# Last stage of a fused block: operands loaded during attention, sigmoids and products reordered, mixes in PSUM, two selects moved

## Chip, cores and metric

The kernel runs on one core of one Trainium2 chip. The metric is the device time in microseconds (us) from the first to the last instruction of the program; lower is better. The times before are three runs of the same kernel, and one further execution was profiled.

## What is computed

The reference is a transformer block on x of shape (4, 2048, 512) in fp32: a layer norm with a modulation computed from a small conditioning vector, causal attention with 16 heads of 32 and a shared rotary part of 32, a gated residual, and then, in the last stage, a second layer norm and a channel-mixing layer with a token shift:

```python
attn = einsum(softmax(causal(scores)), v);  x = x + ga * (attn @ W_o)
h = layernorm(x) * (1 + cb) + sb
h_prev = shift h by one token (0 for the first token of a sequence)
xr = mu_r * h + (1 - mu_r) * h_prev
xk = mu_k * h + (1 - mu_k) * h_prev
r = sigmoid(xr @ W_r.T);  k = square(relu(xk @ W_k.T))
x = x + gb * r * (k @ W_v.T)
```

## The kernel before

Four programs run one after the other, each with its own barrier: setup, projection, attention, feedforward. Every engine's order is written out by hand, with semaphores between engines. A product of two fp32 matrices is made of three matmuls of a high and a low part each (`three_pass`, L59 to L61): high by high, high by low, low by high. The high part is a copy that rounds (made by ACT), the low part the difference (made by DVE or POOL).

**Attention** handles 16 units (4 groups of heads by 4 sequences). A unit has four blocks of 512 queries, j = 0 to 3, with 4, 8, 12 and 16 steps of 128 keys. Per step PE makes scores for four heads (L1005, L1006), ACT the exponentials (L853, into one of five `probs` buffers), PE the weighted values (L1012, two steps at a time, two steps later). POOL sets the future keys of the last four steps of a block to zero (`clear_future`, L929, the "select") and adds the exponentials of most steps into `sum_g` (L954, L957); PE then closes the block's denominators (`att_ps_d`, L1012) from `sum_g`. In block 2, step 8 and step 9 hold the first two selects, and PE waits for both before it takes step 8's and 9's weighted values. In between, PE also makes products for the next unit's row maxima (L991), which DVE reduces.

**Feedforward**, the last stage, turns W_r, W_k and W_v on PE, and splits all four weights into parts; then it walks 16 chunks of 512 tokens. In chunk n PE makes the products r (mix_r by W_r), o (attention by W_o of chunk n+1), k (mix_k by W_k), 16 transposes of the normalised rows of chunk n+1, and v (by W_v): four groups of 12 matmuls in each of r, o, k and v, on four PSUM banks in turn, so that a group waits until its bank was read. The other engines' steps in a chunk:

- ACT: four sigmoids of r (L1339), four copies `keep_x1` (L1329), squares and high parts of k, then the high copies of mix_r of the next chunk, four of the attention (L1317), and the high copies of mix_k (L1323).
- DVE: `attention_out` (L1195), layer norm statistics, relus (L1274), `normalise` (L1211); then `token_shift`: `modulate` (L1225, from the transposes' PSUM banks `ps_t`), `shift` (L1233), `mix` (L1241, into `mix_f` in SBUF) and `mix_low` (L1247), with `value_out` (L1279) between.
- POOL: the product with the gate (L1391), the residual (L1380), the inverse deviation (L1384), low parts of k (L1398), the sum of the output (L1402), low parts of the attention (L1374).
- SP issues every transfer. All loads of the last stage are issued after its barrier, and the gate's load (2 MB, L1154) stands behind four others.

## Time and profile before

| | |
|---|---|
| median of 3 runs | 3795.58 us (3789.31 to 3804.19) |
| profiled execution | 3801.18 us |
| its span, first to last instruction | 3799.4 us |
| mean granted clock of TensorE | 0.969 of full speed |
| busy: PE, DVE, POOL, ACT | 94%, 71%, 72%, 47% of the span |
| attention | until 2915 us of the span |
| last stage | 2915 us to the end |

The span and the time of the profiled execution differ by 1.8 us. Busy shares are means over stages; a matmul's shown end overlaps the next one's start.

### The profile page before, as it was taken

To read this page: it belongs to the slowest core of one execution; us is meant where nothing else is said; L and a number is where in the kernel's file an instruction comes from. 1 tells how busy PE (TensorE), PEld (TensorE's weight loads), DVE (VectorE), ACT (ScalarE), POOL (GpSimd) and SP (SyncE) were. 2 spreads that over 40 slices of the span, in tenths; PEclk is the share of its full clock that TensorE was granted. 3 is DMA by queue.
4 is the path that set the end of the run, shared out by engine and by line. 5 is a ranking of instruction groups with operands and counts; after the bars stand their busy time and mean duration, and the time that the engine had idled before them with its cause. 6 is when DMAs were issued, how large, how long until landed. Compare 5 with 4: busy or idle time off the path is not lost. (4 is left out here: it accounts for less than half of the span.)

```text
span 3799.4 us, 55720 instructions
## 1 busy us (share of the span) xinstructions
PE 3586.7 (94%) x19296; PEld 2423.5 (64%) x19296; DVE 2702.1 (71%) x5390; ACT 1800.5 (47%) x3401; POOL 2722.6 (72%) x1225
## 2 busy tenths in 40 slices
PE   7999979999999999999999999999996899999998
PEld 4777746666666666666666666666663677777776
DVE  5676667777777777777777777777761777777775
ACT  2433325555555555555555555555553333333332
POOL 1333248889889898898898898988986455555555
PEclk8999989999999999999999999999997899999999
DMA  5789753463553544634635635445322111111110
GB/s 182 249 274 301 258 135 79 104 143 76 112 128 78 128 102 100 131 81 106 133 78 107 140 76 119 109 95 128 81 46 98 53 54 66 66 56 66 55 55 33
DMA packets 232263, 425.77 MB, mean 112 GB/s; under 512 B 25332, under 2 KB 26868, under 8 KB 231928
## 3 DMA queue, kind: packets, MB, share of 16 engines
q1 hardware_dynamic: 231992, 423.10, 43.0%
q8 instruction: 117, 1.92, 0.2%
q14 instruction: 90, 0.74, 0.1%
q10 hardware_dynamic: 64, 0.02, 0.0%
HBM read 300.86 MB, written 121.65 MB: 111 GB/s over the span
## 5 line engine op out<-in xcount | busy, mean ns | idle before, releaser
L853 ACT ACTIVATE att_probs<-att_ps_s 128x512 f32<-128x512 f32 (+3 forms) x2560 | 1311.8, 536 | 1014.6 <-PE att_ps_s L1006 915.1
L957 POOL TENSOR_TENSOR att_sum_g<-att_sum_g,att_probs 128x2048 f32<-128x2048 f32 (+3 forms) x432 | 1665.5, 3855 | 57.3 <-ACT att_probs L853 6.9
L888 DVE TENSOR_REDUCE att_piece_max<-att_ps_m 128x1 f32<-128x512 f32 x1536 | 970.8, 683 | 281.1 <-PE att_ps_m L991 278.8
L1005 PE MATMUL att_ps_s<-att_q_a,att_k_a 128*128 128x512 f32 (+3 forms) x2560 | 959.6, 379 | 13.3 <-DMA att_q_b<-att_neg_max 9.2
L1006 PE MATMUL att_ps_s<-att_q_b,att_k_b 65*128 65x512 f32 (+3 forms) x2560 | 932.2, 368 | 0.0
L891 DVE CUSTOM_DVE_ANT_0 att_ps_m<-att_ps_m,mask_qk 128x128 f32<-128x128 f32 (+3 forms) x1024 | 487.4, 512 | 292.5 <-PE att_ps_m L991 276.6
L991 PE MATMUL att_ps_m<-att_k_a,att_q_a 128*128 128x512 f32 (+3 forms) x1840 | 663.3, 383 | 17.1 <-PEq L215 13.7
L1005 PEld LDWEIGHTS att_ps_s<-att_q_a,att_k_a 128*128 128x128 f32 x2560 | 486.4, 190 | 195.1 <-issue 91.1
L1012 PE MATMUL att_ps_o<-att_probs,att_v 128*32 128x512 f32 (+3 forms) x5120 | 561.3, 546 | 32.7 <-POOL att_probs L929 32.7
L1006 PEld LDWEIGHTS att_ps_s<-att_q_b,att_k_b 65*128 65x128 f32 x2560 | 485.7, 190 | 61.2
L991 PEld LDWEIGHTS att_ps_m<-att_k_a,att_q_a 128*128 128x128 f32 x1840 | 348.5, 191 | 235.8 <-issue 105.1
L954 POOL TENSOR_TENSOR att_sum_g<-att_probs 128x1536 f32<-128x1536 f32 (+1 forms) x64 | 276.1, 4314 | 173.0 <-PE att_ps_d L1012 173.0
L1012 PEld LDWEIGHTS att_ps_o<-att_probs,att_v 128*32 128x32 f32 x5120 | 133.9, 110 | 296.3 <-issue 148.6
L901 DVE RECIPROCAL att_ps_d<-att_ps_d 128x128 f32<-128x128 f32 x256 | 224.3, 926 | 91.0 <-PE att_ps_d L1012 91.0
L991 PE MATMUL att_ps_m<-att_k_next,att_q_a 128*128 128x128 f32 (+1 forms) x720 | 256.8, 385 | 0.0
L1402 POOL TENSOR_TENSOR ffn_x_kept<-ffn_x_kept,ffn_gate_r 128x512 f32<-128x512 f32 x64 | 100.5, 1570 | 162.8 <-DVE ffn_gate_r L1279 162.8
L929 POOL TENSOR_SCALAR_AFFINE_SELECT att_probs<-att_probs 128x512 f32<-128x512 f32 x256 | 160.7, 636 | 66.3 <-ACT att_probs L853 66.2
L991 PEld LDWEIGHTS att_ps_m<-att_k_next,att_q_a 128*128 128x128 f32 x720 | 134.3, 190 | 99.8 <-issue 37.7
L1195 DVE TENSOR_TENSOR ffn_x<-ffn_ps_ffn,ffn_gate 128x512 f32<-128x512 f32 x64 | 44.2, 691 | 176.3 <-PE ffn_ps_ffn L61 150.7
L1345 ACT ACTIVATE ffn_act_f<-ffn_relu 128x512 f32<-128x512 f32 x64 | 40.4, 632 | 262.2 <-DVE ffn_relu L1274 261.5
L459 POOL TENSOR_TENSOR prj_h_lo<-prj_h_f,prj_h_hi 128x512 fp32r<-128x512 f32 x64 | 80.5, 1292 | 106.4 <-ACT prj_h_hi L404 106.4
L59 PE MATMUL ffn_ps_ffn<-ffn_w_o_hi,ffn_att_hi 128*128 128x512 f32 x256 | 111.6, 436 | 40.9 <-ACT ffn_gate_r L1339 35.4
(173 smaller groups left out, 5096.8 us busy)
## 6 DMA issues: line engine op xcount, KB each, us to landing
att_q_a<-s_q_hi SPq DMA_DIRECT2D x128, 256.0 KB, 6.0
att_q_a<-s_qr_hi SPq DMA_DIRECT2D x128, 256.0 KB, 7.1
prj_x_sb<-in_x_dram SPq DMA_DIRECT2D x16, 1024.0 KB, 5.3
s_q_hi<-prj_q_hi SPq DMA_DIRECT2D x16, 1024.0 KB, 4.4
s_q_lo<-prj_q_lo SPq DMA_DIRECT2D x16, 1024.0 KB, 6.5
s_k_hi<-prj_k_hi SPq DMA_DIRECT2D x16, 1024.0 KB, 4.5
s_k_lo<-prj_k_lo SPq DMA_DIRECT2D x16, 1024.0 KB, 6.5
s_v<-prj_v_sb SPq DMA_DIRECT2D x16, 1024.0 KB, 9.3
```

What stands on the lines that cost most here:

```text
L59: mm(out, stat[0], mov[0], start=first, stop=False)
L853: act.activation(probs[t % RING][:, hh, c0:CH], ps_s[(GH * t + hh) % SBANKS][:, c0:CH], ACT.Exp, scale=SCALE).then_inc(probs_ready, 1)
L888: dve.tensor_reduce(top, ps_m[:, bank, :], AX_X, ALU.max).then_inc(piece_taken, 1)
L891: dve.tensor_tensor_reduce(ps_m[:, bank, 0:width], ps_m[:, bank, 0:width], keep["mask_qk"][:, CH - width:CH], 1.0, MASKED, ALU.add, ALU.ma ...
L901: dve.reciprocal(cols, cols).then_inc(rden_ready, 1)
L929: pool.affine_select(out=at, in_=at, compare_op=ALU.is_ge, fill=0.0, base=0, pattern=[[0, GH], [1, P]], channel_multiplier=-1).then_inc(cl ...
L954: pool.tensor_tensor(sum_g[:, :, c0:CH], first[:, :, c0:CH], new, ALU.add).then_inc(sum_added, 1)
L957: pool.tensor_tensor(sum_g[:, :, c0:CH], sum_g[:, :, c0:CH], new, ALU.add).then_inc(sum_added, 1)
L991: mm(ps_m[:, bank, 0:width], q_a[j][:, hh, r * P:(r + 1) * P], keys, start=True, stop=True).then_inc(piece_ready, 1)
L1005: mm(out[:, c0:CH], k_a[:, hh, i * P:(i + 1) * P], q_a[j][:, hh, c0:CH], start=True, stop=False)
L1006: last = mm(out[:, c0:CH], k_b[:, hh, i * P:(i + 1) * P], q_b[j][:, hh, c0:CH], start=False, stop=True)
L1012: last = mm(out[hh * HD:(hh + 1) * HD, c0:CH], stat(hh), mov[:, hh, c0:CH], start=start, stop=stop, skip_group_check=True)
```

## The change

1. The four weights of the last stage and the first chunk's attention are loaded by SP during the last unit of attention, into the places of query buffers that this unit no longer needs (`raw_views`, `load_for_last_stage`). Parts of the weights and of the mixes are then kept in attention's operand buffers (keys, queries), so that all fits.
2. The start of the last stage is reordered: W_o is split in four pieces beside the attention's four, PE makes the first two o groups before it turns W_k, and the gate is loaded in four pieces, the first one first.
3. `modulate` goes from DVE to ACT. `mix` writes into `ps_t` (banks 0 and 1 for r, 2 and 3 for k) instead of SBUF.
4. The sigmoids stand between the high copies of mix_k, and no longer wait for the last chunk's output sums; `value_out` writes into the buffers of the relus and squares (`gated`) instead of `gate_r`. The relus and squares take over the wait on those sums.
5. In block 2 of attention, POOL's sum of step 7 stands behind the selects of steps 8 and 9.

```diff
+            def load_for_last_stage(j):
+                wait_alone(sp, scores_ready, GH * (NSTEP * (NU - 1) + FIRST[j] + STEPS[j]), sp_mark)
+                if j == 0:
+                    wait_alone(sp, o_stored, 16 * (TCH * (NU - 2)), sp_mark)
+                    sp.dma_start(ops["raw"]["att"][:], scratch["o"].rearrange("(g n) p t -> n p g t", g=NG)[0]).then_inc(ops["att_in"], 16)
+                    load_weight(0)
+                    load_weight(3)
+                else:
+                    load_weight(j)
...
+                else:
+                    load_for_last_stage(0)
...
+                else:
+                    load_for_last_stage(1)
...
+                else:
+                    load_for_last_stage(2)
...
+                    mine = [n for n, o in enumerate(SHARE_OF[j]) if o == "G"]
+                    order = [(what, i) for i in range(STEPS[j]) for what in ("clear", "add")]
+                    if j == 2:
+                        order.remove(("add", TB * j - 1))
+                        order.insert(order.index(("clear", TB * j + 1)) + 1, ("add", TB * j - 1))
+                    for what, i in order:
+                        if what == "clear" and i >= TB * j:
+                            wait_alone(pool, probs_ready, heads_ready(u, FIRST[j] + i, GH - 1), pool_mark)
                             clear_future(u, j, i)
...
+                        if what == "add" and i in mine[1:]:
+                            add(u, j, i, mine)
...
+        w_o, w_r = ([ops["k_a"][:, k, :].rearrange("p (c n) -> p c n", c=NC) for k in two] for two in ((0, 1), (2, 3)))
+        w_k = ops["k_next"], sb("w_k_lo", [P, NC, D], F32R)
...
+        mix_r, mix_k = (ops["q_a"][0], ops["q_a"][1]), (ops["q_a"][2], ops["q_b"][0])
...
+        w_raw = [ops["raw"][n] for n in ("w_o", "w_r", "w_k", "w_v")]
+        first_att = ops["raw"]["att"]
...
+        gated = [relu[:, 0, :], relu[:, 1, :], act_f[:, 0, :], act_f[:, 1, :]]
...
+            def load_gate(b):
...
+            load_gate(0)
             sp.dma_start(x_sb[:], x_v[0]).then_inc(x_in, 16)
-            sp.dma_start(gate[:], scratch["gate"][None].broadcast_to([P, NB, 2, D])).then_inc(gate_in, 16)
-            load_weight(3)
             sp.dma_start(mu[:, 0, :], dram["mu_r"].rearrange("(c p) -> p c", p=P), allow_slow_non_contiguous=True).then_inc(mu_in, 16)
             sp.dma_start(mu[:, 1, :], dram["mu_k"].rearrange("(c p) -> p c", p=P), allow_slow_non_contiguous=True).then_inc(mu_in, 16)
-            sp.wait_ge(att_lo, NG)
             sp.dma_start(att_f[:], att_v[1]).then_inc(att_in, 16)
+            for b in range(1, NB):
+                load_gate(b)
             sp.wait_ge(x1_ready, TB)
...
+            def output_weight_low(c):
+                dve.wait_ge(wo_hi, c + 1)
+                dve.tensor_tensor(w_o[1][:, c, :], w_raw[0][:, c, :], as_f32(w_o[0][:, c, :]), ALU.subtract).then_inc(wo_lo, 1)
...
-            def modulate(n, c):
-                dve.wait_ge(t_ready, NC * n + c + 1)
-                dve.tensor_scalar(h2[:, c, 1:1 + CH], ps_t[:, c, :], keep["mod"][:, 3, c, bass.ds(n, 1)],
-                                  keep["mod"][:, 2, c, bass.ds(n, 1)], ALU.mult, ALU.add).then_inc(h2_ready, 1)
...
-                dve.scalar_tensor_tensor(out=mix_f[:, c % 2, j, :], in0=diff[:, c, :], scalar=mu[:, j, c:c + 1],
+                dve.scalar_tensor_tensor(out=ps_t[:, 2 * j + c % 2, :], in0=diff[:, c, :], scalar=mu[:, j, c:c + 1],
...
-                dve.tensor_tensor(dst[1][:, c, :], mix_f[:, c % 2, j, :], as_f32(dst[0][:, c, :]),
+                dve.tensor_tensor(dst[1][:, c, :], ps_t[:, 2 * j + c % 2, :], as_f32(dst[0][:, c, :]),
...
-                modulate(n, 0)
                 for c in range(NC):
-                    if c + 1 < NC:
-                        modulate(n, c + 1)
                     shift(n, c)
...
                     dve.wait_ge(actf_ready, NC * n + m - 1)
+                else:
+                    dve.wait_ge(y_ready, TB * n + 1)
                 dve.tensor_scalar(relu[:, m % 2, :], ps[:, m, :], 0.0, None, ALU.max).then_inc(taken[m], 1)
...
+                dve.tensor_tensor(gated[m], ps[:, m, :], gate_r[:, m, :], ALU.mult).then_inc(taken[m], 1)
...
-            weight_low(0)
+            for c in range(NC):
+                output_weight_low(c)
             weight_low(1)
+            dve.wait_ge(gate_in, 16)
+            attention_out(0, range(0, 2))
             weight_low(2)
-            dve.wait_ge(gate_in, 16)
-            attention_out(0)
+            attention_out(0, range(2, TB))
...
+            dve.wait_ge(gate_rest, 16 * (NB - 1))
...
+            def modulate(n):
+                act.wait_ge(carry_ready, n + 2)
+                for c in range(NC):
+                    act.wait_ge(t_ready, NC * n + c + 1)
+                    act.activation(h2[:, c, 1:1 + CH], ps_t[:, c, :], ACT.Identity, scale=keep["mod"][:, 3, c, bass.ds(n, 1)],
+                                   bias=keep["mod"][:, 2, c, bass.ds(n, 1)]).then_inc(h2_ready, 1)
+
+            def gate(n, m):
+                act.wait_ge(*ready(f"r{m}", n))
+                act.activation(gate_r[:, m, :], ps[:, m, :], ACT.Sigmoid).then_inc(taken[m], 1)
...
+                    act.copy(dst[0][:, c, :], ps_t[:, 2 * j + c % 2, :]).then_inc(mix_hi[j], 1)
...
-                for m in range(TB):
-                    act.wait_ge(*ready(f"r{m}", n))
-                    act.wait_ge(y_ready, TB * n + 1)
-                    act.activation(gate_r[:, m, :], ps[:, m, :], ACT.Sigmoid).then_inc(taken[m], 1)
+                for c in range(NC):
+                    mix_high(n, 1, c)
+                    if c:
+                        gate(n, c - 1)
+                gate(n, TB - 1)
...
                 if nxt:
+                    modulate(n + 1)
                     mix_high(n + 1, 0)
                     if after:
                         act.wait_ge(*ready("v3", n))
                         split_attention(n + 2)
-                    mix_high(n + 1, 1)
...
+            act.wait_ge(att_in, 16)
+            for g in range(NG):
+                act.copy(att[0][:, g, :], first_att[:, g, :]).then_inc(att_hi, 1)
+                act.copy(w_o[0][:, g, :], w_raw[0][:, g, :]).then_inc(wo_hi, 1)
+            act.wait_ge(att_lo, NG)
...
+            modulate(0)
             mix_high(0, 0)
             act.wait_ge(grp_ready, 4)
             split_attention(1)
-            mix_high(0, 1)
...
-            pool.wait_ge(gate_in, 16)
-            low_attention(0)
+            low_attention(0, first_att)
...
+            def attention_out(n, reuse, part=range(TB)):
+                if reuse:
+                    pe.wait_ge(att_lo, NG * n + NG)
+                for m in part:
                     if reuse:
                         pe.wait_ge(*bank_free(f"o{m}", n - 1))
                     for c in range(NG):
+                        if not reuse and m == 0:
+                            pe.wait_ge(att_lo, c + 1)
+                            pe.wait_ge(wo_lo, c + 1)
...
-            pe.wait_ge(w_lo, 4)
+
+            turn_weight(1)
+            attention_out(0, False, range(0, 2))
+            turn_weight(2)
+            attention_out(0, False, range(2, TB))
+            turn_weight(3)
+            pe.wait_ge(w_lo, 3)
```

POOL in attention, block 2 of one unit, from the block's first sum on. Before:

```order
L954 TENSOR_TENSOR att_sum_g<-att_probs 128x2048
L957 TENSOR_TENSOR att_sum_g<-att_sum_g,att_probs 128x2048 x6
L929 AFFINE_SELECT att_probs<-att_probs 128x4x128 x2
L957 TENSOR_TENSOR att_sum_g<-att_sum_g,att_probs 128x4x384
L929 AFFINE_SELECT att_probs<-att_probs 128x4x128
L957 TENSOR_TENSOR att_sum_g<-att_sum_g,att_probs 128x4x256
L929 AFFINE_SELECT att_probs<-att_probs 128x4x128
L957 TENSOR_TENSOR att_sum_g<-att_sum_g,att_probs 128x4x128
```

Now:

```order
L982 TENSOR_TENSOR att_sum_g<-att_probs 128x2048
L985 TENSOR_TENSOR att_sum_g<-att_sum_g,att_probs 128x2048 x5
L966 AFFINE_SELECT att_probs<-att_probs 128x4x128 x2
L985 TENSOR_TENSOR att_sum_g<-att_sum_g,att_probs 128x2048
L985 TENSOR_TENSOR att_sum_g<-att_sum_g,att_probs 128x4x384
L966 AFFINE_SELECT att_probs<-att_probs 128x4x128
L985 TENSOR_TENSOR att_sum_g<-att_sum_g,att_probs 128x4x256
L966 AFFINE_SELECT att_probs<-att_probs 128x4x128
L985 TENSOR_TENSOR att_sum_g<-att_sum_g,att_probs 128x4x128
```

The two selects of 128x4x128 have gone ahead of one full sum.

ACT in the last stage, from the head of the loop over chunks to the end of the sigmoids. Before (the first row is the last in front of the loop, and the same at the end of its body):

```order
L1323 CAST ffn_mix_k_hi<-ffn_mix_f 128x512 x4
L1364 UNCONDITIONAL_BRANCH
L1364 ISA
L1338 ISA
L1339 ACT_TABLE_LOAD
L1339 ACTIVATE ffn_gate_r<-ffn_ps_ffn 128x512
L1337 REGISTER_ALU
L1339 ACTIVATE ffn_gate_r<-ffn_ps_ffn 128x512
L1337 REGISTER_ALU
L1339 ACTIVATE ffn_gate_r<-ffn_ps_ffn 128x512
```

Now, where `att_q_a<-ffn_ps_t` is the high copy of mix_k:

```order
L1422 UNCONDITIONAL_BRANCH
L1422 ISA
L1375 ACT_TABLE_LOAD
L1375 CAST att_q_a<-ffn_ps_t 128x512
L1374 REGISTER_ALU
L1375 CAST att_q_a<-ffn_ps_t 128x512
L1368 ISA
L1369 ACT_TABLE_LOAD
L1369 ACTIVATE ffn_gate_r<-ffn_ps_ffn 128x512
L1374 REGISTER_ALU
L1375 CAST att_q_a<-ffn_ps_t 128x512
L1368 REGISTER_ALU
```

The copies of mix_k have come from the end of the loop's body to its head, the sigmoids stand between them, and there are two loads of a function table where there was one.

DVE in the loop, the first part of `token_shift`. Before:

```order
L1225 ISA
L1225 TENSOR_SCALAR ffn_h<-ffn_ps_t,mod 128x512
L1225 ISA
L1225 TENSOR_SCALAR ffn_h<-ffn_ps_t,mod 128x512
L1233 TENSOR_TENSOR ffn_diff<-ffn_h 128x512
L1241 SCALAR_TENSOR_TENSOR ffn_mix_f<-ffn_diff,ffn_mu,ffn_h 128x512
L1225 ISA
L1225 TENSOR_SCALAR ffn_h<-ffn_ps_t,mod 128x512
L1233 TENSOR_TENSOR ffn_diff<-ffn_h 128x512
L1247 TENSOR_TENSOR ffn_mix_r_lo<-ffn_mix_f,ffn_mix_r_hi 128x512
L1241 SCALAR_TENSOR_TENSOR ffn_mix_f<-ffn_diff,ffn_mu,ffn_h 128x512
```

Now:

```order
L1272 TENSOR_TENSOR ffn_diff<-ffn_h 128x512
L1280 SCALAR_TENSOR_TENSOR ffn_ps_t<-ffn_diff,ffn_mu,ffn_h 128x512
L1272 TENSOR_TENSOR ffn_diff<-ffn_h 128x512
L1286 TENSOR_TENSOR att_q_a<-ffn_ps_t,att_q_a 128x512
L1280 SCALAR_TENSOR_TENSOR ffn_ps_t<-ffn_diff,ffn_mu,ffn_h 128x512
L1315 REGISTER_ALU
L1317 TENSOR_TENSOR ffn_relu<-ffn_ps_ffn,ffn_gate_r 128x512
```

The modulations (L1225) have left DVE's order, and the mixes go to `ffn_ps_t`.

## Rows read from the trace of the kernel before

**Rows 1.** Timeline, block 2 of one unit of attention: start, duration, engine, operation, [idle before].

```profile
1907.50 1.07 PE L1012 MATMUL att_ps_d<-att_sum_g,ones 128*32 128x512 f32 x8 [0.36 <-POOL att_sum_g L957]
...
1913.47 28.26 POOL L957 TENSOR_TENSOR att_sum_g<-att_sum_g,att_probs 128x2048 f32<-128x2048 f32 x6
...
1931.69 4.56 ACT L853 ACTIVATE att_probs<-att_ps_s 128x512 f32<-128x512 f32 x8 [2.37 <-PE att_ps_s L1006]
...
1941.69 1.22 POOL L929 TENSOR_SCALAR_AFFINE_SELECT att_probs<-att_probs 128x512 f32<-128x512 f32 x2
1942.38 1.06 PE L1012 MATMUL att_ps_o<-att_probs,att_v 128*32 128x512 f32 x8 [1.75 <-POOL att_probs L929]
...
1950.18 1.29 POOL L957 TENSOR_TENSOR att_sum_g<-att_sum_g,att_probs 128x512 f32<-128x512 f32 x1
...
1953.10 1.07 PE L1012 MATMUL att_ps_d<-att_sum_g,ones 128*32 128x512 f32 x8
```

**Rows 2.** Timeline of PE, that wait in four of fifteen units, first and last included.

```profile
758.30 1.41 PE L1012 MATMUL att_ps_o<-att_probs,att_v 128*32 128x512 f32 x8 [1.74 <-POOL att_probs L929]
...
1054.52 1.06 PE L1012 MATMUL att_ps_o<-att_probs,att_v 128*32 128x512 f32 x8 [1.74 <-POOL att_probs L929]
...
1201.84 1.21 PE L1012 MATMUL att_ps_o<-att_probs,att_v 128*32 128x512 f32 x8 [1.78 <-POOL att_probs L929]
...
2838.41 1.94 PE L1012 MATMUL att_ps_o<-att_probs,att_v 128*32 128x512 f32 x8 [1.77 <-POOL att_probs L929]
```

**Rows 3.** Window: engines' busy us, granted clock, DMA share, GB/s.

```profile
2835.00:2840.00 5.00, 3.23 (x19) 1.72 (x23) 0.50 (x2) 1.83 (x7) 4.92 (x4) 0.76 0.01 2
```

**Rows 4.** Chain that ended last and timeline, start of the last stage.

```profile
2915.02 0.39 SPq L1146
...
2919.25 17.71 DMA ffn_gate<-s_gate
...
2937.03 4.94 POOL L1374 TENSOR_TENSOR ffn_att_lo<-ffn_att_f,ffn_att_hi 128x512 fp32r<-128x512 f32 x4 [30.67 <-DMA ffn_gate<-s_gate]
...
2963.69 3.64 PE L1446 MATMUL ffn_ps_t<-ident_f,ffn_diff 128*128 128x128 f32 x16 [6.25 <-DVE ffn_diff L1211]
```

**Rows 5.** Timeline of PE, one chunk of the last stage.

```profile
3062.89 1.91 PE L1446 MATMUL ffn_ps_t<-ident_f,ffn_diff 128*128 128x128 f32 x16
...
3075.82 0.39 PE L59 MATMUL ffn_ps_ffn<-ffn_w_r_hi,ffn_mix_r_hi 128*128 128x512 f32 x1
...
3080.38 0.50 PE L59 MATMUL ffn_ps_ffn<-ffn_w_r_hi,ffn_mix_r_hi 128*128 128x512 f32 x1 [2.20 <-DVE ffn_mix_r_lo L1247]
...
3088.68 0.39 PE L59 MATMUL ffn_ps_ffn<-ffn_w_r_hi,ffn_mix_r_hi 128*128 128x512 f32 x1
...
3091.76 0.48 PE L59 MATMUL ffn_ps_ffn<-ffn_w_o_hi,ffn_att_hi 128*128 128x512 f32 x1 [2.24 <-ACT ffn_gate_r L1339]
...
3113.94 1.91 PE L1446 MATMUL ffn_ps_t<-ident_f,ffn_diff 128*128 128x128 f32 x16
```

**Rows 6.** Timeline of PE, transposes of the second and the last chunk.

```profile
3010.50 1.91 PE L1446 MATMUL ffn_ps_t<-ident_f,ffn_diff 128*128 128x128 f32 x16
...
3740.64 1.91 PE L1446 MATMUL ffn_ps_t<-ident_f,ffn_diff 128*128 128x128 f32 x16
```

**Rows 7.** Timelines of DVE, ACT and POOL, same chunk.

```profile
3075.39 1.78 DVE L1247 TENSOR_TENSOR ffn_mix_r_lo<-ffn_mix_f,ffn_mix_r_hi 128x512 fp32r<-128x512 f32 x1
...
3083.36 6.82 POOL L1374 TENSOR_TENSOR ffn_att_lo<-ffn_att_f,ffn_att_hi 128x512 fp32r<-128x512 f32 x4
...
3089.72 1.28 ACT L1339 ACT_TABLE_LOAD   x1
3091.01 2.07 ACT L1339 ACTIVATE ffn_gate_r<-ffn_ps_ffn 128x512 f32<-128x512 f32 x4
```

**Rows 8.** Groups by line, 3000 to 3700 us: count, busy us, mean ns.

```profile
L1225 DVE TENSOR_SCALAR ffn_h<-ffn_ps_t,mod 128x512 f32<-128x512 f32 x56 | 43.9, 805 | 2.9 <-DVE ffn_h L1219 2.9
...
L1279 DVE TENSOR_TENSOR ffn_gate_r<-ffn_ps_ffn,ffn_gate_r 128x512 f32<-128x512 f32 x53 | 36.0, 679 | 0.0
```

More of the change, by code:

```diff
@@ L668, in operand_loads, with attention @@
     return load_q_a, load_q_b, load_k_a, load_k_b, load_v, (heads, rotary)
-def attention(nc, keep, scratch, ops):
+def attention(nc, keep, scratch, ops, dram):
     with ExitStack() as ctx:
@@ L680, in attention @@
         k_b = sb("k_b", [2 * HD + 1, GH, T], F32R)
-        ops["q_a"] += [sb(f"q_a{j}", [P, GH, CH], F32R) for j in range(2, TCH)]
+        ops["q_a"].append(sb("q_a3", [P, GH, CH], F32R))
         ops["q_b"] += [sb(f"q_b{j}", [2 * HD + 1, GH, CH], F32R) for j in range(1, TCH)]
@@ L1428, in token_rows @@
                 last.then_inc(grp_ready, 1)
-            def attention_out(n, reuse):
-                pe.wait_ge(att_lo, NG * n + NG)
-                for m in range(TB):
+            def attention_out(n, reuse, part=range(TB)):
+                if reuse:
+                    pe.wait_ge(att_lo, NG * n + NG)
+                for m in part:
                     if reuse:
@@ L1525, in adaln_block @@
                 projection(nc, keep, dram, scratch, prj, ops)
-            attention(nc, keep, scratch, ops)
-        feedforward(nc, keep, dram, scratch, out)
+            late_operands(nc, held, ops)
+            ops["raw"] = raw
+            attention(nc, keep, scratch, ops, dram)
+            feedforward(nc, keep, dram, scratch, out, ops)
 _INS = {
```

115 lines of the change are left out of this document (56 added, 59 removed).

## The prediction

> **What bounds the kernel now.** I read three stretches in the timeline, each for the wait that PE ends last, since PE is busy nearly everywhere else.
>
> First, attention. In every unit from the second on, PE stands still for 1.75 us in front of the weighted values of block 2's steps 8 and 9, released by POOL's select [rows 1, 2]; there are fifteen such waits, from 758.30 to 2838.41. POOL came to the selects late because it had six full sums to make first (28.26 us). The exponentials that the selects need were done at 1931.69 + 4.56 = 1936.25, long before the select at 1941.69. The mean distance of two such waits is (2838.41 - 758.30) / 14 = 148.6 us, but 1201.84 - 1054.52 = 147.3 where the clock held. In most units the granted clock falls around this wait (0.76 in one window [rows 3]), that is, part of it goes at 1.2 instead of 2.4 GHz, and the same eight matmuls take up to 1.94 instead of 1.06 us [rows 1, 2].
>
> Second, the start of the last stage. From its first transfer at 2915.02 to the first chunk's transposes at 2963.69 it takes 48.7 us [rows 4]. The chain of waits shows why: the gate's transfer took 17.71 us behind the weights, POOL waited for it before the attention's low parts (4.94 us), and only then did PE begin the products o.
>
> Third, the chunks. From the second chunk's transposes to the last one's, 3010.50 to 3740.64, are 14 periods of 52.15 us [rows 6]. In the chunk shown [rows 5] the period is 3113.94 - 3062.89 = 51.05. The r groups run from 3075.82 to the last triple's end at 3088.68 + 0.69, that is 13.55 us, where 16 triples without a wait take 11.1 (o and k together, 32 triples, take 3113.94 - 3091.76 = 22.2): 2.45 lost, waiting for mix_r's low part on DVE. Then o starts at 3091.76 instead of 3089.37: 2.4 lost, waiting for the sigmoid, which ACT starts only behind all copies of mix_k and a table load of 1.28 us [rows 7]. Without both the chunk takes 46.2 us. The other 1.1 us of the mean are longer waits of the same two kinds and the lower clock after them.
>
> **The change, part by part.** The sum is made against the profiled execution's own 3801.2 us.
>
> *Selects in block 2.* POOL's sixth full sum is put behind the selects. The full sum lasts 28.26 / 6 = 4.7 us, so the selects start at about 1937.0, when the exponentials are 0.8 us old: POOL loses nothing, and the selects are over at 1938.3, two us before PE asks (1942.38 - 1.75 = 1940.6). The stall of 1.75 goes. Next is late what closes block 2: POOL's last sum ends at 1950.18 + 1.29 = 1951.5, PE's closing product was at 1953.10 and would now be at 1951.35, so PE waits there as it does for block 1 (0.36 [rows 1]). Net 1.75 - 0.35 = 1.4 by 15 units = 21 us. The clock: 148.6 - 147.3 = 1.3 us a unit, 19 us in all; it goes if the falls hang on this stall, and I take nine tenths, 17. Together **38 us**. The bounds are 5 (if POOL's sums set the pace all through) and 45.
>
> *Loads during attention.* Five transfers of 1 MB go into the last unit, where the DMA engines are idle (share 0.01 [rows 3]). SP issues them where it otherwise loads the next unit's queries, so they stand ahead of two stores and two small loads of row maxima that other units have behind larger loads. Cost nothing; if this cover were gone, at most the gate's 17.7 us of one transfer queue.
>
> *Start of the last stage.* From 2915: four pairs of copies on ACT at 0.55 us (2.07 / 4 [rows 7]) end at 2919.7, POOL's low parts of the attention at about 2920.5 (4.94 in sequence), while PE turns W_r. The o products, which began at 2942, can begin at 2919.2: 22.8 us earlier. What followed them took 21.7 us until the transposes, and now has W_k's turning in it as well (1.9 us [rows 5], the copy and difference behind it lie beside the next products). I take 2942.7, **21 us** earlier. Bounds 15 (the gate's first quarter or SP's slow small loads of mu late) and 24.
>
> *Chunks, DVE.* Four modulations of 0.80 us leave the stretch that gates r [rows 8]. The low parts now read one operand from PSUM: with two operands in SBUF they took 1.78 us while a POOL sum ran [rows 7], with PSUM on one side, as in value_out, the mean of 53 is 0.68 whatever POOL did [rows 8]. I followed the order by hand from the transposes (T): mix 0 is ready at T + 4.3; each further step is shift, low, mix and value_out at 0.6 to 0.7 each, plus some 0.6 of waiting for POOL, 3.3 in all; the last low part ends at T + 14.4. PE needs it at T + 12.9 + 2.1 = 15.0 (transposes and v, 3075.82 - 3062.89 [rows 5], and three quarters of the first r group). The stall closes, with 0.6 us to spare. For a modulation on ACT the nearest row, the sigmoids from PSUM, has 2.07 / 4 = 0.52 us [rows 7]; the upper bound is DVE's 0.80 [rows 8]. Four of them start when ACT is through with the squares of k, about 2.3 us into the transposes, and only the first is waited for. The Trainium skill (ScalarE: Activation LUTs, What ACT_TABLE_LOAD costs) adds some 93 ns for each of the two pointer operands; by that it is 0.79, no more than the upper bound.
>
> *Chunks, ACT and POOL.* The sigmoid of r0 now follows the second copy of mix_k. The copies run at T + 18.9 and T + 19.7, the table load ends at T + 21, the sigmoid at T + 21.6; PE comes to o at T + 12.9 + 11.1 = 24.0. No wait. What is late next is POOL: it adds the last output sum at T + 19 or so and then makes four low parts of the attention, which took 6.82 us with DVE in between [rows 7] and about 5.9 with fewer DVE operations of two SBUF operands. That gives T + 24.2 to 25, so I leave 0.2 to 1.0 us of waiting. Row maxima of mix_k, relus and squares keep their distances to k, which has 11 us in hand; the store of the last output has some 6 us to land before `keep_x1`. Period 46.2 + 0.6 = 46.8 us; 14 periods save 5.35 each, **75 us**. Bounds: 5.95 each (83 us) and 1.5 each (21 us).
>
> A rule weighed here: the row shows the table load at 1.28 us and the sigmoids starting at once behind it, at 3091.01 [rows 7]. The order now has two such loads per chunk, 2.6 us of ACT. The Trainium skill (same page and section) counts 2.66 us for every switch of sets, the drain included. By the row the sigmoid has 2.4 us in hand before o; by the page it would come 2.8 us later, o would wait 0.4 us and the 14 periods save some 6 us less.
>
> *Ends.* The first chunk gains about 1.5 us (shorter steps on DVE), the last one its wait for mix_r of the same kind as above and the clock behind it, 3 us. Together **4.5 us**.
>
> Sum: 38 + 21 + 75 + 4.5 = 138.5, so 3801.2 - 138.5 = 3662.7. The median of the runs lies 5.6 us below the profiled execution: **3657 us**, 3.6% faster.
>
> **Rivals.**
>
> *A, POOL becomes the wait in the chunks.* POOL's low parts of the attention follow the output sum, which follows value_out of v3, which DVE reaches late, and every DVE operation with two SBUF operands stretches POOL's. For it speaks that POOL ended at 3083.36 + 6.82 = 3090.2, only 1.6 us before o was released by the sigmoid; against it that DVE gets there earlier. If PE waits 2.5 us each chunk and the clock takes 0.5 more, a period is 49.2: 41 us instead of 75, and the time 3691.
>
> *B, the selects bring nothing.* POOL is the pace of block 2 and its closing eats the stall: 5 us instead of 38, time 3690. For it speaks that closings of block 1 already wait for POOL; against it that this wait is 0.36 and that PE had 1.6 us in hand at block 2's [rows 1].
>
> *C, both*: 3724.
>
> *D, slower: ACT holds r back.* Modulations and copies of mix_r are now in one line on ACT, behind the squares of k. If its operations on PSUM banks that DVE writes were so slow that the chain of four modulations and four copies grew, PE would wait for mix_r in every chunk. The other terms give 63.5 us; to be slower by 0.5% (19 us) the chunks have to lose 82.5 / 14 = 5.9 us each against now, so the chain has to be some 12 us longer than I have it, 1.5 us for each of its eight operations. That would give 3815. The rows show 0.5 to 0.8 for such operations.
>
> *E, no change over 0.5%*: the waits only change their names, period and units alike; 3780 to 3795.
>
> **How the numbers follow.** Chances: forecast 0.60 (its own range 3632 to 3680), A 0.18, B 0.12, C 0.05, D 0.03, E 0.02. The predicted time is that of the forecast, 3657. The low end takes all upper bounds, 45 + 24 + 83 + 6 = 158: 3801.2 - 158 - 5.6 = 3637.6, and a little for the scatter of the runs, 3634. The high end takes in A and B with some margin and stops short of C: 3706. Below 0.5% (19 us) the runs of this kernel, which differ by 15 us, could hardly tell a change. Faster by more than that: forecast and A to C, 0.95; same 0.02; slower 0.03.
>
> **What would show it.** PE's wait before `att_ps_o` in block 2 is gone in units 2 to 16, and one of 0.3 us stands before `att_ps_d` of block 2; the distance of units is 146 us with the clock at full speed there. The first transposes of a chunk come 28 us behind the start of the last stage. The periods of the transposes are 46 to 47.5 us, and the wait before o, if any, names POOL's low parts of the attention, not the sigmoid. Wrong would be: a wait for mix_r still over 1 us in each chunk (my steps on DVE), a wait named after ACT's modulations, POOL standing idle in front of block 2's selects, or clock falls in other places of attention.

## The result, and the profile after

The changed kernel takes 3670.07 us (median of 4 runs, 3669.48 to 3673.73), and the kernel before, run beside it, 3792.44 us: a ratio of 0.9674, 95% interval 0.9651 to 0.9698. The profiled execution took 3669.48 us (span 3667.7), 131.7 us less than that of before; the prediction had 138.5.

The page of the changed kernel, busy time by engine and the granted clock in 40 slices:

```profile
PE 3536.2 (96%) x19296; PEld 2400.9 (65%) x19296; DVE 2577.7 (70%) x5329; ACT 1855.2 (51%) x3482; POOL 2711.1 (74%) x1225
...
PEclk8999979999999999999999999999999899999999
```

The timeline of block 2 of the unit shown in [rows 1], POOL and PE, from the closing of block 1 to that of block 2:

```profile
1903.96 1.06 PE L1054 MATMUL att_ps_d<-att_sum_g,ones 128*32 128x512 f32 x8 [0.36 <-POOL att_sum_g L985]
...
1905.20 4.61 POOL L982 TENSOR_TENSOR att_sum_g<-att_probs 128x2048 f32<-128x2048 f32 x1 [1.38 <-PE att_ps_d L1054]
1909.95 23.55 POOL L985 TENSOR_TENSOR att_sum_g<-att_sum_g,att_probs 128x2048 f32<-128x2048 f32 x5
1933.44 1.23 POOL L966 TENSOR_SCALAR_AFFINE_SELECT att_probs<-att_probs 128x512 f32<-128x512 f32 x2
1934.63 8.20 POOL L985 TENSOR_TENSOR att_sum_g<-att_sum_g,att_probs 128x2048 f32<-128x2048 f32 x2
...
1945.84 0.64 POOL L966 TENSOR_SCALAR_AFFINE_SELECT att_probs<-att_probs 128x512 f32<-128x512 f32 x1
1946.54 0.43 PE L1054 MATMUL att_ps_o<-att_probs,att_v 128*32 128x128 f32 x8 [1.04 <-POOL att_probs L966]
...
1947.89 1.06 PE L1054 MATMUL att_ps_d<-att_sum_g,ones 128*32 128x512 f32 x8 [0.43 <-POOL att_sum_g L985]
...
1949.13 4.60 POOL L982 TENSOR_TENSOR att_sum_g<-att_probs 128x2048 f32<-128x2048 f32 x1 [1.30 <-PE att_ps_d L1054]
```

The wait of 1.75 us ahead of steps 8 and 9 is gone. Two others stand in its place, 1.04 us for the select of step 11 and 0.43 for the last sum, and between 1905.20 and the last sum POOL is never idle. In the kernel before POOL wasn't idle there either. Its timeline of a unit in which the clock held shows PE closing 0.05 us behind the last sum (1062.36 + 1.28), and the same 1.30 us between that sum and the next block:

```profile
1020.83 4.61 POOL L954 TENSOR_TENSOR att_sum_g<-att_probs 128x2048 f32<-128x2048 f32 x1 [1.38 <-PE att_ps_d L1012]
...
1062.36 1.28 POOL L957 TENSOR_TENSOR att_sum_g<-att_sum_g,att_probs 128x512 f32<-128x512 f32 x1
1063.69 1.07 PE L1012 MATMUL att_ps_d<-att_sum_g,ones 128*32 128x512 f32 x8
1064.94 4.60 POOL L954 TENSOR_TENSOR att_sum_g<-att_probs 128x2048 f32<-128x2048 f32 x1 [1.30 <-PE att_ps_d L1012]
```

I measure block 2 below from its first sum on POOL to that of block 3: 1064.94 - 1020.83 = 44.11 us here, 43.93 after. Over fifteen units (all but the first) before had 44.1 us in four and 45.0 to 46.9 in eleven (mean 45.35); after has 43.9 to 44.3 in thirteen and 44.8 in two (mean 44.10).

The start of the last stage and the chunks, timeline of SP's queue and PE, answering to [rows 4, 6]:

```profile
2898.74 0.33 SPq L1191 DMA_DIRECT2D ffn_gate<-s_gate  x1
...
2902.09 0.78 PE L59 MATMUL ffn_ps_ffn<-att_k_a,ffn_att_hi 128*128 128x512 f32 x1
...
2926.16 3.65 PE L1509 MATMUL ffn_ps_t<-ident_f,ffn_diff 128*128 128x128 f32 x16 [6.25 <-DVE ffn_diff L1255]
...
2970.02 1.91 PE L1509 MATMUL ffn_ps_t<-ident_f,ffn_diff 128*128 128x128 f32 x16
...
3613.23 1.91 PE L1509 MATMUL ffn_ps_t<-ident_f,ffn_diff 128*128 128x128 f32 x16
```

From first transfer to first transposes are 27.4 us (48.7 before), and a period of the chunks is (3613.23 - 2970.02) / 14 = 45.94 us (52.15 before). PE has no wait left in these 14 periods, and the granted clock is 1.00 in all of them. One chunk on ACT, POOL and PE, in timelines as [rows 7]:

```profile
3077.47 1.28 ACT L1375 ACT_TABLE_LOAD   x1
3078.76 1.07 ACT L1375 CAST att_q_a<-ffn_ps_t 128x512 fp32r<-128x512 f32 x2
3079.65 5.94 POOL L1432 TENSOR_TENSOR ffn_att_lo<-ffn_att_f,ffn_att_hi 128x512 fp32r<-128x512 f32 x4
3079.85 1.28 ACT L1369 ACT_TABLE_LOAD   x1
3081.15 0.60 ACT L1369 ACTIVATE ffn_gate_r<-ffn_ps_ffn 128x512 f32<-128x512 f32 x1
...
3085.73 0.42 PE L59 MATMUL ffn_ps_ffn<-att_k_a,ffn_att_hi 128*128 128x512 f32 x1
...
3110.03 2.78 ACT L1364 ACTIVATE ffn_h<-ffn_ps_t,mod 128x512 f32<-128x512 f32 x4
```

and DVE's groups by line over the chunks (2970 to 3613 us), the low parts of mix_r and mix_k:

```profile
L1286 DVE TENSOR_TENSOR att_q_a<-ffn_ps_t,att_q_a 128x512 fp32r<-128x512 f32 x56 | 38.4, 685 | 1.7
L1286 DVE TENSOR_TENSOR att_q_b<-ffn_ps_t,att_q_a 128x512 fp32r<-128x512 f32 x56 | 38.3, 684 | 11.8 <-ACT att_q_a L1375 10.9
```

POOL's low parts end at 3079.65 + 5.94 = 3085.59, 0.14 us before PE begins the products o at 3085.73.

### The profile page after: what moved, and what is told of

Its sections match the earlier page's. It is cut to its first block and busy times, and to the rows that moved or that the text cites. A ratio compares the mean times of both kernels' runs of the same rounds, so it can differ in the third digit from the quotient of the medians.

```text
span 3667.7 us, 55764 instructions
## 1 busy us (share of the span) xinstructions
PE 3536.2 (96%) x19296; PEld 2400.9 (65%) x19296; DVE 2577.7 (70%) x5329; ACT 1855.2 (51%) x3482; POOL 2711.1 (74%) x1225
## 3 DMA queue, kind: packets, MB, share of 16 engines
q1 hardware_dynamic: 232424, 423.10, 44.1%
## 5 line engine op out<-in xcount | busy, mean ns | idle before, releaser
L1033 PE MATMUL att_ps_m<-att_k_a,att_q_a 128*128 128x512 f32 (+3 forms) x1840 | 663.7, 383 | 17.0 <-PEq L215 13.7
L1239 DVE TENSOR_TENSOR ffn_x<-ffn_ps_ffn,ffn_gate 128x512 f32<-128x512 f32 x64 | 44.1, 691 | 159.7 <-PE ffn_ps_ffn L61 159.7
L928 DVE DVE_READ_ACCUMULATOR2_ANT att_piece_max<- 128x1 f32 x1024 | 144.1, 141 | 0.0
L1456 POOL TENSOR_TENSOR ffn_att_lo<-ffn_act_f,ffn_att_hi 128x512 fp32r<-128x512 f32 x64 | 86.0, 1354 | 68.1 <-ACT ffn_att_hi L1385 68.1
```

The costliest lines, as they stand in the source:

```text
L928: dve.tensor_tensor_reduce(ps_m[:, bank, 0:width], ps_m[:, bank, 0:width], keep["mask_qk"][:, CH - width:CH], 1.0, MASKED, ALU.add, ALU.ma ...
L1033: mm(ps_m[:, bank, 0:width], q_a[j][:, hh, r * P:(r + 1) * P], keys, start=True, stop=True).then_inc(piece_ready, 1)
```

## Where the 131.7 us are

| stretch | predicted | measured | from |
|---|---|---|---|
| attention, from unit 1's block 3 to the end | 38 | 18.3 | 2293.6 and 2275.3 us |
| ahead of that | 0 | -2.0 | block 3 of unit 1 starts at 621.45 before, 623.49 after |
| start of the last stage | 21 | 21.3 | 48.7 and 27.4 us |
| 14 periods | 75 | 86.9 | 52.15 and 45.94 us |
| first and last chunk | 4.5 | 7.2 | 46.8 and 43.9; 58.8 and 54.5 us |

The 2.0 us ahead aren't the change's: that block started between 621.4 and 623.8 us in all executions profiled, whatever they contained.

My theory of attention (P) from here on: POOL's chain of sums and selects sets the pace of block 2, before and after; moving the selects only moves PE's pause, and what it gained is the clock. The rivals are the prediction's step (PE sets the pace) and C (the clock falls have another cause).

## The experiments

Ratios are against the kernel before, run on the same chip; "from the changed kernel" compares medians of separate sets of runs.

| run | median us | ratio, 95% interval | from the changed kernel |
|---|---|---|---|
| select_only (on before) | 3774.09 | 0.9952, 0.9936 to 0.9967 | |
| select_back | 3692.46 | 0.9722, 0.9691 to 0.9752 | +22 |
| last_selects | 3675.01 | 0.9683, 0.9657 to 0.9709 | +5 |
| step11_on_pe | 3635.81 | 0.9582, 0.9557 to 0.9606 | -34 |
| step11_only | 3653.53 | 0.9622, 0.9584 to 0.9659 | -17 |
| modulate_dve | 3692.21 | 0.9737, 0.9710 to 0.9765 | +22 |
| mix_sbuf | 3711.41 | 0.9788, 0.9760 to 0.9816 | +41 |
| sigmoids_last | 3672.88 | 0.9686, 0.9658 to 0.9713 | +3 |
| both_back | 3729.84 | 0.9826, 0.9788 to 0.9864 | +60 |
| all_back | 3761.38 | 0.9905, 0.9875 to 0.9935 | +91 |
| loads_late | 3680.28 | 0.9707, 0.9679 to 0.9734 | +10 |
| gate_whole | 3671.70 | 0.9674, 0.9636 to 0.9713 | +2 |

### The selects alone, and the selects back

select_only is the kernel before with POOL's order of the change (the functions `add` and `body` of the diff) and nothing else. select_back is the changed kernel without it:

```diff
-                    if j == 2:
-                        order.remove(("add", TB * j - 1))
-                        order.insert(order.index(("clear", TB * j + 1)) + 1, ("add", TB * j - 1))
```

> The kernel before with only the order of POOL in block 2 changed (the sum of step 7 behind the selects of steps 8 and 9). Theory P, POOL's chain of sums and selects (42.6 us from its first sum) sets the pace of block 2, and only the clock falls hang on the order: block 2, from POOL's first sum to that of block 3, takes 43.95 us in nearly all units instead of 44.1 to 46.9, PE waits some 1.1 us for the select of step 11 and 0.4 for the last sum, and the time is 18 us below the kernel before (2 for the stall, 16 for the clock). The prediction's own step, PE was the pace and the stall falls away: 38 us below. Rival C, the clock falls come from elsewhere and were gone in the changed kernel for another reason: 2 us below, with falls in most units.

> The changed kernel with only the order of POOL in block 2 put back (sum of step 7 ahead of the selects). Theory P: the 1.75 us stall before steps 8 and 9 is back, block 2 takes 44.1 us where the clock holds and 45.3 to 46.9 where it falls, 16 to 20 us above the changed kernel, all of it in attention; the chunks stay at 45.94 us. The prediction's step: 38 us above. Rival C (the falls have another cause): 2 us above.

select_only came 20.8 us below the median of before, block 2 at 43.95 to 43.98 us in twelve of fifteen units (mean 44.11, before 45.35: 15 x 1.24 = 18.6 us). Its timeline has the two small waits of the changed kernel:

```profile
1946.10 0.43 PE L1017 MATMUL att_ps_o<-att_probs,att_v 128*32 128x128 f32 x8 [1.07 <-POOL att_probs L929]
...
1947.45 1.06 PE L1017 MATMUL att_ps_d<-att_sum_g,ones 128*32 128x512 f32 x8 [0.44 <-POOL att_sum_g L948]
```

select_back lost 22 us, and block 2 was back at 45.3 to 46.8 in thirteen units (mean 45.85). The prediction's step (38 each way) and C (2) are out. P fits: 18 expected and 20.8 measured without the other edits, 16 to 20 expected and 22 measured among them. In select_back's trace the clock fell in fourteen of the fifteen units, where before it had in eleven. The windows of select_back around one of its pauses, engines' busy time, granted clock, DMA share and GB/s, show the clock's part:

```profile
1650.00:1655.00 5.00, 3.32 (x24) 2.11 (x26) 1.08 (x4) 2.36 (x8) 4.92 (x4) 0.79 0.31 88
1655.00:1660.00 5.00, 5.00 (x24) 1.66 (x17) 0.00 (x0) 0.03 (x1) 4.92 (x3) 0.53 1.06 210
```

In the second window PE is busy throughout (5.00 of 5 us), at little more than half of the full clock (0.53).

### The pause moved, and POOL relieved

last_selects also exchanges the select of step 11 with the sum of step 10; step11_only leaves that order and gives the sum of step 11 to PE; step11_on_pe does both.

```diff
+                        order.remove(("add", TB * j + 2))
+                        order.insert(order.index(("clear", TB * j + 3)) + 1, ("add", TB * j + 2))
```

```diff
-SHARE_OF = ("GGTT", "GGGGGGGG", "GGGGGGGGTGGG", "GGGGGGTGGGGGTGGG")
+SHARE_OF = ("GGTT", "GGGGGGGG", "GGGGGGGGTGGT", "GGGGGGTGGGGGTGGG")
```

> The changed kernel with one more pair of POOL's operations in block 2 exchanged: the select of step 11 ahead of the sum of step 10. POOL's work in the block is the same, so theory P expects block 2 at 43.95 us as in the changed kernel: the wait of 1.08 us at the select goes, and PE waits 1.5 us for the last sum instead (now 0.44). If the clock holds, the time is that of the changed kernel within 3 us. If one pause of 1.5 us in one piece is what lets the clock fall (it was 1.75 us before, in one piece), falls come back in many units and the time is up to 16 us above. The rival that this select's place costs PE time by itself: 1.1 us a unit less, 16 us below.

> As the run with the last selects exchanged, and in addition the sum of step 11 of block 2 is made by PE (four products of 128 columns, some 0.25 us) and not by POOL (1.29 us). Theory P: block 2 gets 1.2 to 1.3 us shorter, 42.7 us, PE's waits shrink to 0.3 us or less, and 15 or 16 units give 19 us, so 19 us below the changed kernel. The rival that PE is the pace of block 2 (the prediction's step): 4 us above the changed kernel.

> The changed kernel with the sum of step 11 of block 2 on PE, but the selects in the changed kernel's order (select of step 11 behind the sum of step 10). Theory P: PE still waits about 1 us for that select, but closes right behind: block 2 takes 43.2 us (43.95 in the changed kernel, 42.47 with both edits), and the 0.75 us a unit that block 3 got shorter through the new deal of the maxima stays. Together 1.4 to 1.5 us a unit, 22 us below the changed kernel, 12 above the kernel with both edits. The rival that the whole gain of the kernel with both edits comes from the sum's place and the deal: 34 us below.

last_selects: the select's wait is gone, and the closing waits instead, in one piece of 1.61 to 1.70 us in nine of the fifteen units (0.57 to 1.27 in the five before them, 3.29 in the last):

```profile
1945.40 1.06 PE L1056 MATMUL att_ps_d<-att_sum_g,ones 128*32 128x512 f32 x8 [1.66 <-POOL att_sum_g L985]
```

Block 2 takes 43.9 us where the clock holds, as without the exchange, so the same work on POOL gives the same time wherever PE pauses. The clock fell behind this closing in five units, and in two of them block 3 took 65.8 us for 62.8. These 6 us are about what the kernel lost (5 us).

step11_on_pe shows who sets the pace. POOL has a sum of 1.28 us less, PE the second row below more, and block 2 takes 42.47 us, 1.5 less. PE comes to the closing just when POOL is done (1200.11 + 2.38 = 1202.49) and closes without a wait:

```profile
1200.11 2.38 POOL L985 TENSOR_TENSOR att_sum_g<-att_sum_g,att_probs 128x1024 f32<-128x1024 f32 x1
...
1201.78 0.40 PE L1056 MATMUL att_ps_d<-att_probs,ones 128*32 128x128 f32 x8
...
1202.55 1.07 PE L1056 MATMUL att_ps_d<-att_sum_g,ones 128*32 128x512 f32 x8
```

The direction is P's, the size wasn't: 34 us for 19. Block 2 gave 23.3 us over fifteen units. The rest is block 3, 62.05 for 62.8 us, 0.75 in each unit, although POOL and PE do the same work there. The share table (`SHARE_OF`, which engine sums which step) also feeds the plan that deals the products for the row maxima to the steps, and in the new deal one of them stands between two heads of step 1 of block 3, where PE before followed ACT's pace. That this is the cause is read from the timelines only, no run has the new deal alone. step11_only has the shorter block 3 too (62.1), without the exchange. Its block 2 takes 43.58 us (I had 43.2), and it gains 17 us for the 22 that I expected, since PE still waits 0.93 us for the select of step 11:

```profile
1205.62 0.43 PE L1054 MATMUL att_ps_o<-att_probs,att_v 128*32 128x128 f32 x8 [0.93 <-POOL att_probs L966]
```

So both edits count, and their worth hangs on POOL's chain: the exchange of step 11's select costs 5 us by itself, and on top of the shorter chain it brings 18. step11_on_pe is 0.9% faster than the changed kernel and the fastest version I have.

### The chunks: modulation, mixes, sigmoids

Each run undoes one part of the changed kernel.

```diff
             def token_shift(n, meanwhile):
+                modulate(n, 0)
                 for c in range(NC):
+                    if c + 1 < NC:
+                        modulate(n, c + 1)
                     shift(n, c)
```

is modulate_dve, with `modulate` as in the kernel before. mix_sbuf writes and reads the mixes in a buffer of their own:

```diff
-                    act.copy(dst[0][:, c, :], ps_t[:, 2 * j + c % 2, :]).then_inc(mix_hi[j], 1)
+                    act.copy(dst[0][:, c, :], mix_f[:, 2 * j + c % 2, :]).then_inc(mix_hi[j], 1)
```

and so in `mix` and `mix_low`. sigmoids_last has `gate_r` for `gated`, and:

```diff
-                for c in range(NC):
-                    mix_high(n, 1, c)
-                    if c:
-                        gate(n, c - 1)
-                gate(n, TB - 1)
+                mix_high(n, 1)
+                act.wait_ge(y_ready, TB * n + 1)
+                for m in range(TB):
+                    gate(n, m)
```

> The changed kernel with the modulation put back on DVE (one ahead of each shift, as before). My step order: DVE's stretch from the transposes to the last low part of mix_r gets four modulations of 0.7 to 0.8 us more and starts 0.4 us earlier, less 0.8 us of waiting that they fill, so the last low part comes about 1.5 to 2 us later; it has 0.7 us in hand, so PE waits about 1 us for it in each chunk and the period grows from 45.94 to about 47 us: 15 us above the changed kernel. In addition the attention's low parts on POOL, which end 0.1 us before PE begins the products o, shift with DVE's value_out, but PE shifts as well. The rival that the modulation's move is the largest part of the chunks' gain: 3 us each, period 49, 43 us above. The rival that it brings nothing beside the mixes in PSUM: 0.

> The changed kernel with the mixes kept in SBUF and not in the PSUM banks of the transposes, so that each low part has two SBUF operands. If such an operation waits for the whole operation of POOL that runs beside it (1.78 us in the trace of before against 0.68 with one PSUM operand), each of the four low parts of mix_r takes 0.5 to 1.1 us longer: 3 us later at the end, of which 0.7 are in hand, so PE waits 2.3 us before r in each chunk, and POOL, held up too, comes later with the attention's low parts by some 1 us: period 48.5 us, 36 us above the changed kernel, with clock falls. If the two operands don't matter: period 45.94, no change.

> The changed kernel with the sigmoids put back behind all four copies of mix_k, into the buffer that value_out then overwrites, behind the wait for the last output sum. The copies now come earlier than in the kernel before: the fourth ends 13.1 us before the next transposes minus 35.2, that is 21.9 us behind the chunk's transposes, the table load ends at 23.2 and the first sigmoid at 23.8, when PE is through with r at 23.9 (0.1 us in hand). My theory: PE waits 0 to 0.3 us, period 45.9 to 46.2, 0 to 4 us above the changed kernel, so the place of the sigmoids brings next to nothing once the mixes come early. The prediction's reading (a part of 2.4 us a chunk hangs on this order): 34 us above.

Periods: 47.39, 48.82 and 46.15 us against 45.94, that is 1.45, 2.88 and 0.21 us a chunk. I had 1, 2.5 and 0 to 0.3, so the first two are dearer than expected, and the clock falls that I expected with the mixes in SBUF didn't come (1.00 in all 14 periods). In the timelines PE waits, with the modulation on DVE, 0.55 us for mix_r and 0.33 for POOL's low parts; with the mixes in SBUF:

```profile
3132.96 0.50 PE L59 MATMUL ffn_ps_ffn<-att_k_a,att_q_a 128*128 128x512 f32 x1 [1.56 <-DVE att_q_a L1287]
...
3142.83 0.50 PE L59 MATMUL ffn_ps_ffn<-att_k_a,ffn_att_hi 128*128 128x512 f32 x1 [0.74 <-POOL ffn_att_lo L1433]
```

The reason stands in mix_sbuf's groups by line (2970 to 3650 us), the same low parts with both operands in SBUF, and POOL's low parts of the attention beside them:

```profile
L1287 DVE TENSOR_TENSOR att_q_b<-ffn_mix_f,att_q_a 128x512 fp32r<-128x512 f32 x56 | 93.8, 1694 | 3.6 <-ACT att_q_a L1376 3.6
L1287 DVE TENSOR_TENSOR att_q_a<-ffn_mix_f,att_q_a 128x512 fp32r<-128x512 f32 x56 | 85.0, 1518 | 2.4
```

```profile
L1433 POOL TENSOR_TENSOR ffn_att_lo<-ffn_att_f,ffn_att_hi 128x512 fp32r<-128x512 f32 x56 | 95.6, 1737 | 0.0
```

Only the place of one operand differs, and the instruction takes 1518 to 1694 ns for 685, POOL's 1737 for the 1518 of the changed kernel. It isn't that SBUF is slow to read: the same instruction is short where POOL is idle and long where POOL runs, here in one chunk of mix_sbuf:

```profile
3121.92 0.69 DVE L1287 TENSOR_TENSOR att_q_a<-ffn_mix_f,att_q_a 128x512 fp32r<-128x512 f32 x1
...
3123.95 1.68 POOL L1461 TENSOR_TENSOR ffn_x_kept<-ffn_x_kept,ffn_relu 128x512 f32<-128x512 f32 x1 [4.06 <-DVE ffn_relu L1318]
3124.39 1.79 DVE L1287 TENSOR_TENSOR att_q_a<-ffn_mix_f,att_q_a 128x512 fp32r<-128x512 f32 x1
```

Over thirteen chunks mix_r's low parts take 0.69 us the 13 times that POOL is idle and 1.78 to 1.82 the 39 times that it runs; in the changed kernel, with one operand in PSUM, they take 0.67 to 0.69 either way. The Trainium skill (SBUF — State Buffer, Who interferes with whom) has this as a rule: a DVE instruction with two SBUF inputs contends with a GpSimd instruction that reads SBUF, and one with a single SBUF input, outside its two-port modes, doesn't. The trace agrees, with these numbers. The sigmoids' place is worth 0.21 us by itself, as the copies of mix_k now come early.

### The same parts, undone together

both_back undoes modulation and mixes, all_back the sigmoids too, with the same edits.

> The changed kernel with both edits on DVE's side undone, the modulation on DVE and the mixes in SBUF; the sigmoids stay between the copies of mix_k. Alone the two cost 1.45 and 2.88 us a chunk (periods 47.39 and 48.82 against 45.94). Theory S, one chain through DVE with 0.7 us in hand: the delays add up and the slack is only paid once, so both together cost about 1.45 + 2.88 + 0.7 = 5.0, period 51.0 us, 70 us above the changed kernel, unless the clock falls, which adds up to 1. The rival that the edits stand in for each other (either would do): 48.8 to 49.3.

> As the run with modulation and mixes put back, and the sigmoids behind all copies of mix_k too: the chunk schedule of the kernel before on top of the other edits. Theory S: since the copies of mix_k are late now, the sigmoid is late for the products o, and what was worth 0.2 us alone is worth 1 to 2 here: period 52.1 us as in the kernel before (52.15), with clock falls in most chunks. The rival that the order of the sigmoids is worth 0.2 everywhere: period as in the run with the sigmoids between the copies, plus 0.2.

both_back has a period of 49.84 us, 3.90 above the changed kernel; the single losses add to 4.33. So the parts don't stand in for each other, and the slack doesn't count once more on top, as I had expected (51.0). Five of its periods hold a clock fall (50.2 to 51.1 us); the other nine take 49.5, 3.6 above. Why the two together cost less than their sum isn't shown. all_back has 52.10 us, near the kernel before's 52.15, so the other edits bring nothing to a chunk. The sigmoids' order is worth 52.10 - 49.84 = 2.26 us here and 0.21 in the changed kernel: PE's wait in all_back's timeline is the one of [rows 5], longer:

```profile
3107.26 0.47 PE L59 MATMUL ffn_ps_ffn<-att_k_a,ffn_att_hi 128*128 128x512 f32 x1 [3.27 <-ACT ffn_gate_r L1378]
```

The chunk of [rows 5] isn't the common one. In the kernel before PE waits for mix_r either 1.1 or 2.2 us, and o begins 28.8 us behind the transposes in thirteen of the 14 periods whichever it was: the sigmoid sets that moment, and a longer first wait only makes the second one shorter. Nor do the two waits add to more in any other period than to the 4.4 us of that chunk. What lifts the mean to 52.15 is the clock: twelve of the 14 periods hold a fall, and [rows 5] shows one of the other two.

### The start of the last stage

loads_late issues them in the last stage's queue, and none in attention:

```diff
+            load_weight(1)
+            load_weight(0)
+            sp.dma_start(first_att[:], att_v[0]).then_inc(att_in, 16)
             load_gate(0)
+            load_weight(2)
             sp.dma_start(x_sb[:], x_v[0]).then_inc(x_in, 16)
+            load_weight(3)
```

gate_whole loads the gate at once, in the place of `load_gate(0)`:

```diff
+                sp.dma_start(gate[:], scratch["gate"][None].broadcast_to([P, NB, 2, D])).then_inc(gate_in, 16)
...
-            for b in range(1, NB):
-                load_gate(b)
```

> The changed kernel with the first attention rows and the four weights loaded at the start of the last stage and not in the last attention unit; the gate still comes in parts, and POOL doesn't wait for it. W_r, W_o and the attention rows need 3 MB; their transfers took 5.6, 8.4 and 8 us from issue to landing in the trace of before, one behind the other, so the products o begin about 11 us behind the start of the stage and not 3.3: the stretch from its first transfer to the first transposes grows from 27.4 to about 35 to 37 us, 8 to 10 us above the changed kernel. The rival that the loads' early place is worth the whole 21 us: 48 us, 21 above. The rival that only POOL's wait for the gate mattered: 28 us, no change.

> The changed kernel with the gate loaded in one transfer of 2 MB and not in four of 512 KB. DVE needs the gate for the first two o groups 11.7 us behind the start of the stage (2910.40 against 2898.74); the whole gate took 17.7 us in the trace of before behind 4 MB of others, and here has the queue to itself at first: some 10 to 14 us. So DVE comes up to 2 us late for o0, which must be taken for the residual, not for PE's next products; x and the small loads of mu land later too, and the last token shift waits for mu. First transposes 27.4 to 31 us behind the start, 0 to 4 us above the changed kernel. The rival that the split carries the start's gain: 17.7 us for the gate, 6 us or more.

loads_late: from its first transfer at 2896.24 to the first transposes at 2934.75 are 38.5 us, 11.1 more (I had 35 to 37 us); o begins 13.7 us in and not 3.3. The last unit of attention takes 148.9 us from its first sum without the loads and 149.7 with them, so they cost attention little (0.8 us between these two runs). Its timeline of PE:

```profile
2901.90 3.67 PE L1530 MATMUL ffn_ps_t<-ident_f,raw_w_r 128*128 128x128 f32 x16 [12.36 <-DMA raw_w_r<-in_w_r_dram]
2909.96 0.77 PE L59 MATMUL ffn_ps_ffn<-att_k_a,ffn_att_hi 128*128 128x512 f32 x1 [4.38 <-DVE att_k_a L1216]
```

gate_whole: 2923.38 - 2895.95 = 27.4 us, no change. So of the 21.3 us at the start 11 hang on the loads in attention. The other 10 are left for POOL no longer waiting for the gate and for the order of the steps; no run parts these two. With the loads in attention, one piece of the gate or four makes no difference.

## Why the prediction held, and where it didn't

**The time** was in the range, 13 us above the predicted one. Against the profiled executions I was 6.8 us off, and that is luck in part: the selects were 19.7 us too high, the periods and the ends together 14.6 too low. The rest of the 13 is mostly the 5.6 us by which I put the median under the profiled execution of before; the changed kernel's runs lie within 4 us, and its median 0.6 above its profiled execution.

**Selects in block 2** is the step that failed: 38 us predicted, 18.3 measured. Its clock part was right (17; block 2 got 45.35 - 44.10 = 1.25 us shorter on average, 0.13 where the clock held, so 15 x 1.12 = 17 are the clock's). Its stall part was "Net 1.75 - 0.35 = 1.4 by 15 units = 21 us", and it is 2. It rests on "PE had 1.6 us in hand at block 2's [rows 1]": POOL's last sum ended at 1951.5 and PE closed at 1953.10. But that row is from a unit in which the clock had fallen behind the stall, and PE was late for that reason. In the four units with the clock up PE closes 0.05 us behind POOL's last sum, before as after (1063.69 above): PE had nothing in hand. I took the clock's loss once as clock and once as slack. Rival B, which I gave 0.12, had the mechanism right and the price wrong, for it gave up the clock's gain too. Both runs of the selects and step11_on_pe show it. "POOL loses nothing" was right, and for that reason the move could give nothing.

**Loads during attention** at nothing: it is at most some 0.8 us, the difference of two single units. The start at 27.7 us and 21 saved: 27.4 and 21.3, right.

**Chunks.** Mechanism right, size too small: 75 against 86.9, beyond the bound of 83. I had mix_r's last low part at T + 14.4 (measured 14.2), the modulations between 0.52 and 0.80 (0.70 each, 2.78 for four), the sigmoid at T + 21.6 (19.9). Wrong were two small terms: I left 0.2 to 1.0 us for POOL's low parts, which end 0.14 us ahead of PE and cost nothing (0.6 x 14 = 8 us), and the period without its waits is 45.94, not 46.2 (4 us). My bound counted the waits as printed, and these don't hold all that PE loses: mix_sbuf's two add to 2.3 us and its chunk is 2.88 longer. The shares of the parts weren't as I read them off the two waits (2.45 for r, 2.4 for the sigmoid): undone one by one they are 2.88 for the mixes, 1.45 for the modulation, 0.21 for the sigmoids, and 6.15 all together. The two waits had one cause, DVE's late mixes: the copies of mix_k wait for them, and the sigmoids stood behind these copies. With the mixes early the old order of the sigmoids costs 0.21 us.

**Table loads.** Two in each chunk of the loop, each 1.28 us, and the next operation starts 0.01 us behind (3077.47 + 1.28 and 3078.76). By the rule of the Trainium skill (ScalarE: Activation LUTs, What ACT_TABLE_LOAD costs), 2.66 us with the drain, that copy would come 1.4 us later; the trace doesn't show it, in none of the last stage's 28 loads. For the modulation the same section's figures (186 ns, 0.833 ns for each of the 512 columns, 93 ns for each of the two pointer operands, less 93 ns of overlap) give an estimate of 0.71 us, and the 0.70 measured agrees; the 0.79 of the prediction left the overlap out.

**Ends.** 7.2 for 4.5. The last chunk gave 4.3 for 3. The first gave 2.9 for 1.5, and about half of that is this execution's luck: it took 43.9 us here and 44.7 to 45.6 in the six other runs with the same chunks, against 46.8 in the kernel before and 46.5 in select_only.

**Rivals.** A didn't come, by 0.14 us, which no working could have told; with either part of DVE's relief undone it does (0.33 and 0.74 us a chunk). D and E didn't.

## What to carry to other kernels

- Before a stall is priced as a gain, follow the engine that released it over a whole period: if it is never idle from one release to the next, it is the pace, and another order only moves the pause. Take slack only from a stretch where the clock is up, or the same loss is counted twice.
- Two waits on different engines can have one cause further up; what a part is worth is told by undoing it alone and then together (0.21 and 2.26 us for the same order of sigmoids).
- Where DVE and POOL share a stretch, a PSUM bank that stands free is a better place for an intermediate than SBUF: the place of the mixes was worth 2.9 us of a 46 us chunk.

## What the hardware showed that I had not expected

The longer PE's single pause in block 2, the more often the granted clock fell from 2.4 to 1.2 GHz behind it. With pauses of 1.68 to 1.78 us it fell in 11 of 15 units (before) and 14 of 15 (select_back), with 1.61 to 1.70 in four of nine (last_selects), with 1.04 to 1.08 and 0.44 us apart in two of eleven (changed kernel, whose last unit had 2.3 us and a fall), and shorter ones went with no fall in these runs. The chunks stood longer pauses: 1.6 and 0.7 us left the clock at 1.00 throughout (mix_sbuf). In both_back a first pause of 2.2 us went with a fall in four of eight chunks, 1.1 and 1.75 us in one of six; in all_back 2.2 us in four of four and 3.3 us in eight of ten. So the length of the pause alone doesn't decide it. What else does is open.
